# Six scatters of edge features in flight in place of four, and one wait per chunk for layer 1's row gathers

## The reference, cut to what matters

```python
edge_index = stack([src, dst])
x = layernorm(x + L0(x))   # hypergraph convolution: two rounds of two segment sums, relu between
x = layernorm(x + L1(x, edge_attr_64))
x = layernorm(x + L2(x))   # gate = sigmoid(k[dst] + q[src]); segment sum of gate * v[src]
x = layernorm(x + L3(x))   # normalised segment sum of x[col]

# L1, the layer that reads the features of the edges
edge_in = concat([edges, nodes[receivers], nodes[senders]])      # receivers = src, senders = dst
h = relu(edge_in @ We1 + be1)
new_edges = h @ We2 + be2
agg = segment_sum(new_edges, receivers)
new_nodes = relu(concat([agg, nodes]) @ Wn1 + bn1) @ Wn2 + bn2
```

## Time and profile before

| | us |
|---|---|
| median of 3 runs | 4566.49 |
| lowest, highest | 4554.29, 4575.78 |
| the profiled execution, its own time | 4560.08 |
| its span in the profile | 4558.5 |

### The profile page before, as it was taken

How to read it: one execution, slowest core, us unless ns; L and a number is a source line. 1 busy time by engine, 2 the same in 40 slices (tenths; PEclk the granted TensorE clock), 3 DMA queues, 4 the chain that set the end, 5 groups by cost and what they waited for, 6 DMA issues and landing times.

```text
span 4558.5 us, 127255 instructions
## 1 busy us (share of the span) xinstructions
PE 3684.6 (81%) x48218; PEld 3255.3 (71%) x48218; DVE 2888.4 (63%) x3816; ACT 1600.4 (35%) x2668; POOL 2574.3 (56%) x2291
## 2 busy tenths in 40 slices
PE   0777699998899998378999999999766777777396
PEld 0656588887899997357777777777655767767396
DVE  6999888887111102268888888888545666666502
ACT  0333399997000000223333333333224544444200
POOL 0288866666555656677777777777203444444100
PEclk9776799999999999689999999999888999999798
DMA  5611188888999997568888888888517767767596
GB/s 163 241 30 30 43 305 319 322 324 325 340 387 385 418 416 279 172 210 267 273 273 275 272 271 272 274 260 274 190 38 240 264 231 239 252 235 247 166 407 249
DMA packets 430076, 1159.85 MB, mean 254 GB/s; under 512 B 111175, under 2 KB 250422, under 8 KB 422712
## 3 DMA queue, kind: packets, MB, share of 16 engines
q1 hardware_dynamic: 331478, 919.45, 56.8%
q0 software_dynamic: 66016, 114.12, 8.4%
q10 hardware_dynamic: 32256, 121.34, 6.8%
HBM read 791.79 MB, written 364.93 MB: 254 GB/s over the span
## 4 chain that ended last, share of the span: by engine, by line
DMA 33%; issue 25%; POOL 17%; PE 16%; DVE 5%; POOLq 2%; SPq 1%; ACT 1%; DVEq 0%; ACTq 0%
DMA feat_slot<-SK,sidx_p 19%; DMA arena<-tab_l_src,SK 7%; POOL arena L854 7%; POOL feat_slot L930 5%; PE PS L1271 4%; POOL arena L973 4%; PE PS L1396 3%; PE PS L1376 2%; DMA sidx_p<-SK 2%; PE PS L1370 2%; DMA arena<-feat_slot 2%; DMA hots<-arena 1%; PE PS L1365 1%; PE PS L1342 1%; DMA SK<-in_edge_attr_dram 1%
## 5 line engine op out<-in xcount | busy, mean ns | idle before, releaser
L930 POOL DMA_INDIRECT feat_slot<-SK,sidx_p x900 | 1106.8, 1230 | 557.0 <-DMA feat_slot<-SK,sidx_p 283.6
L973 POOL DMA_INDIRECT arena<-tab_l_src,SK x864 | 1007.9, 1167 | 266.8 <-issue 216.8
L854 POOL TENSOR_TENSOR arena<-arena 128x448 f16<-128x448 f32 x343 | 363.2, 1059 | 660.6 <-ACT arena L1730 660.5
L1271 PE MATMUL PS<-arena 128*128 128x192 bf16 (+1 forms) x7203 | 615.6, 248 | 104.3 <-DVE arena L2183 62.2
L1271 PEld LDWEIGHTS PS<-arena 128*128 128x128 bf16 x7203 | 606.7, 98 | 111.7 <-DVE arena L2183 62.5
L1438 PE MATMUL PS<-arena 128*128 128x128 f16 x4802 | 459.8, 223 | 134.4 <-DVE arena L2364 73.8
L1442 PE MATMUL PS<-arena 128*128 (+1 forms) x4802 | 439.0, 195 | 0.1
L1438 PEld LDWEIGHTS PS<-arena 128*128 128x128 bf16 x4802 | 313.1, 99 | 161.8 <-issue 147.4
L2429 DVE TENSOR_TENSOR arena<-arena 128x896 f32<-128x896 f32 (+1 forms) x319 | 328.1, 1028 | 150.3 <-ACT arena L1770 136.7
L1370 PE MATMUL PS<-arena 128*128 (+1 forms) x4178 | 418.6, 224 | 0.0
L1396 PE MATMUL PS<-arena 128*128 128x384 bf16 x2089 | 416.7, 337 | 2.1 <-DVE arena L2436 2.1
(11 more groups left out here) (274 smaller groups left out, 6546.6 us busy)
## 6 DMA issues: line engine op xcount, KB each, us to landing
arena<-slot_rows SPq DMA_DIRECT2D x343, 448.0 KB, 5.6
arena<-cnt_t SPq DMA_DIRECT2D x147, 896.0 KB
hots<-arena ACTq DMA_DIRECT2D x175, 672.0 KB
arena<-hots SPq DMA_DIRECT2D x175, 672.0 KB, 4.3
arena<-cnt_t SPq DMA_DIRECT2D x147, 672.0 KB
cnt_t<-arena SPq DMA_DIRECT2D x49, 1568.0 KB
cnt_s<-arena SPq DMA_DIRECT2D x49, 1568.0 KB
arena<-cnt_s SPq DMA_DIRECT2D x49, 896.0 KB
```

What stands on the lines that cost most here:

```text
L854: pool.tensor_tensor(halves[i][:, n:2 * n], gated[i], halves[i][:, 0:n], ALU.subtract).then_inc(msg_lo, 1)
L930: pool.indirect_dma_start(feat_slot, bass.IndirectOffsetOnAxis(ap=sidx_p[odd][:, n:n + 1].bitcast(u32), axis=0), fwin[h][:, t * D:(t + 1) ...
L973: pool.indirect_dma_start(qgot[n % 3][:, slot_of[t] * P:(slot_of[t] + 1) * P], None, tab_src[4], bass.IndirectOffsetOnAxis(ap=gidx[odd][:, ...
L1271: last = nc.tensor.matmul(PS[:, at:at + w3], ring[u % RING][:, of:of + P], esplit[:, (i * CH + w) * w3:(i * CH + w + 1) * w3], start=u == ...
```

## The change

`LIVE` goes from 4 to 6: six scatters may be in flight, with six semaphores of 6 landings a window each. The gathers of layer 1 get two semaphores in place of six, one for even and one for odd chunks. Before its first gather, a chunk waits once, on the semaphore of its own parity, until the whole chunk two before has landed. The wait before each gather and the empty instruction behind it go, and `add_sources` waits once for the whole chunk.

```diff
-LIVE = 4
+LIVE = 6
 PUTS = WT // LIVE
...
-        q_in = added[4:7] + [gate_in, gate_out, ft_in]
+        q_in = added[4:6]
...
                         if n == 0:
                             pool.wait_ge(gidx_in, j * 16 + 16)
+                        if not first or n >= 2:
+                            pool.wait_ge(q_in[n % 2], (j * NCH + n - n % 2) * (TN * 8))
                         pool.nop(nofuse=True)
                         for t in range(TN):
                             tile = n * TN + t
-                            if not first or n > 0:
-                                pool.wait_ge(q_in[t], j * (NCH * 16) + n * 16)
-                                pool.nop(nofuse=True)
                             pool.indirect_dma_start(qgot[n % 3][:, slot_of[t] * P:(slot_of[t] + 1) * P], None, tab_src[4],
                                                     bass.IndirectOffsetOnAxis(ap=gidx[odd][:, tile:tile + 1].bitcast(u32), axis=0))\
-                                .then_inc(q_in[t], 16)
+                                .then_inc(q_in[n % 2], 16)
...
-                    for t in range(TN):
-                        dve.wait_ge(q_in[t], j * (NCH * 16) + (c + 1) * 16)
+                    dve.wait_ge(q_in[c % 2], (j * NCH + c - c % 2 + 2) * (TN * 8))
```

## The result

The changed kernel takes 4524.69 us, the median of 9 runs (4512.89 to 4544.69); the kernel before, in the same runs, 4559.55 (9 runs, 4552.73 to 4585.29). The ratio is 0.9916, 95% interval 0.9896 to 0.9936: faster by 0.84%, some 38 us (29 to 47); the medians lie 34.9 apart. Forecast were 4512 us, 4490 to 4548, and "faster by over 0.5%" at 82 in 100. The time lies in the range, 13 us above the forecast. The profiled execution took 4529.34 us.

A forecast was written before the change was run, and what follows sets the result against it. The prediction took POOL, issuing gathers end to end, to bound layer 1. Its terms, -56.6 (earlier gathers) + 2 (layer 0) + 0 (gathers' edit) = -54.6 us, took the 4566.5 us median to 4512, range 4490 to 4548.

The forecast's parts named there:

- 1780 to 1880: Sign in the changed kernel's profile: layer 0's scatters end between 1780 and 1880 us.
- the 1814 of the sum: Predicted end of the scatters: near 1944 us less some 130 us of waits that go.
- what the sum took at nothing: Excess scatter waits after 1815 us, and those before 560 us, were not counted as savings.
- only wait longer: Rival: scatters wait their turn behind bulk stores, so six in flight gain 0, time 4566 us; 12 in 100.
- The next thing late: Layer 1's gathers cannot start before its tables are split (`splits_lo`, about 1890.7 us), bounding the gain at 56.6 us.
- layer 0 +2: Term for layer 0: scatters and fetches moved ahead of 1800 us delay it by 2 us.
- the bound of 13: Most that layer 0 loses if loads bound it: some 13 us of transfers moved earlier.
- the 10 us that it named as a sign of being wrong: Sign against the prediction: layer 0 ending more than 10 us later.
- costs nothing: Term for layer 1's gathers: their new chunk-wise wait and the removed waits and empty instructions together change 0 us.
- cover enough: Waiting for the chunk two before leaves 9.1 us of cover, against gather landings of at most 7.4 us.
- to pace layer 1: POOL issues layer 1's gathers end to end and PE follows, so start delays or gains reach the end in full.
- -56.6: Term for the earlier start of layer 1's gathers: 1947.29 - 1890.73 = 56.6 us saved, taken in full.

The follow-up runs named there:

- e3: The changed kernel with a wait and an empty instruction put back before each gather, on the chunk's own semaphore and count: 4527.83 us, ratio 0.9930.
- e7: The changed kernel with a second load of the same source indices per pair, into a tile nobody reads: 4516.07 us (1 run).
- e2: The changed kernel with four scatters in flight in place of six, so the gathers' edit alone: 4572.9 us, ratio 1.0019.
- e1: The kernel before with six scatters in flight in place of four, gathers as before: 4508.39 us, ratio 0.9893.
- e12: The changed kernel with four semaphores for the gathers in place of two, three gathers to each, waits once a chunk: 4501.73 us, ratio 0.9885.
- e5: The changed kernel with twelve semaphores for the gathers in place of two, one for each of up to twelve unfinished: 4513.10 us, ratio 0.9885.
- e4: The changed kernel with the load of the next pair's source indices issued after the fourth chunk in place of the second: 4532.52 us (1 run).
- e10: The changed kernel without the source-index loads from the third pair on, so layer 1's sums differ: 4526.0 us (1 run).
- e11: The changed kernel with three loads of the source indices per pair, two into tiles nobody reads: 4523.38 us (1 run).

## Why the prediction was right, and where it was not

*The scatters.* Right in mechanism and nearly in size. The waits for their own landings nearly go, other waits come in their place, and the last scatter falls inside 1780 to 1880, 24 us earlier than the 1814 of the sum. Most of these 24 us are what the sum took at nothing: behind 1815 the kernel before has another 16 us of waits over the gaps of 0.30 (39.6 us before 79 scatters). That six in flight would "only wait longer" is ruled out by the series 3, 4, 6, 9, in which the time to landing does not grow: the landings seen beside layer 0's loads are latencies that more scatters cover, not the rate at which a full queue serves. From 1400 to 1600 us, where the DMA share reads 1.02, POOL is busy for 135.4 us with scatters where it was 119.0. The Trainium skill (DMA: Bandwidth & Descriptors, "Queues, rings and completion order") has the queues of a DMA engine take turns by packets; the runs do not show the turns, but if there are any they leave room for this.

*The start of the gathers.* The next thing late was the split of the tables, as forecast, and POOL's path to it was shortened past need: of 153.8 us 105.5 end as a wait.

*Layer 0.* The term "layer 0 +2" was too small. Its last reduction comes at 1794.37; in the timeline of before the same one stands at 1787.14, so +7.2; in the other profiles with six or nine scatters in flight it is between 1792.9 (e3) and 1798.0 (e7). That is 6 to 11 us, inside the bound of 13 that the prediction set by the moved transfers, and at its upper end past the 10 us that it named as a sign of being wrong. PE's waits for `cnt_t` from 1110 to 1800 us hardly grew (42.0 to 42.9 us), so the loss is spread thinly and which instruction bears it was not followed.

*The gathers.* This is the step that failed: that the gathers' edit "costs nothing". The prediction asked whether looser waits could let POOL fall behind and found cover enough, and treated the semaphore on which a landing is counted as free. Measured, the edit puts 27 us into the gathers' stretch of the profile, and some 9 to 20 us into the time: 9 by e2's ratio and 13 by the medians of e2 and before, 10 by the ratios of the change and e1 and 16 by their medians, 14 by the ratios of the change and e12, 20 by the spans of the change and e1.

The runs narrow down the cause so far. Shown: it is not the instruction stream (e3) and not the number that may be unfinished (e5, e12, both with twelve and no standstill); with the same chunk-wise wait and the same bound it is there with six gathers on a semaphore and not with three (e12); it stands right behind the load of the indices, moves with it (e4), and is absent without that load (e10) and with two or three of them (e7, e11). Four profiles of four have it with six gathers on a semaphore and one load a pair; each of the kernels without it was profiled once. Open: why POOL stands, and what is counted over three pairs, 108 gathers and 3 loads, so that every third load meets it (all but one in e2). Not shown either is what POOL waits for: in the changed kernel, in the 2 us after it goes on, 17, 3, 2, 0, 1 and 0 landing events of its DMAs come at the six places, where 18 are usual, so in five of six it goes on about when nearly all that it had issued has landed. A simple count of DMAs since the last standstill was the idea behind e7, e10 and e11; it wanted standstills at other distances there, and none came.

*What the standstills cost.* The prediction took POOL to pace layer 1, from the earlier trace rows, and for lost time that holds: the stretch of 1311.3 us is 30 to 31 us longer than in e5 and e12 (1280.9 and 1280.1), which have the same bound of twelve, and the standstills are 29.1. Against before's 1284.6 it is 27. It would not hold for time saved: in e10, relieved of its loads and its standstills, POOL waits for DVE.

*The sum, put right:* -50.5 for the start (layer 0's share in it), +26.7 for the gathers, -7.0 behind them, which is within what that part differs by between profiles. The prediction's own working with 7 for layer 0 gives -56.6 + 7 + 0 = -49.6, and e1, which has no gathers' edit, measured -51. Of the forecast -54.6 the change brought 35 by medians, 38 by the ratio. The step that failed is the "+ 0" for the gathers, with the "+ 2" for layer 0 too small by 5. That the time came out only 13 us above 4512, and not 20, is luck of the base: the median of the three runs shown, 4566.5, lies 7 us above that of the nine.

## What to carry to other kernels

Waits for a transfer's own landing go away with more in flight as long as the landing is latency; count what the next dependency leaves of the gain before you count the waits (here 51 of 157 us), and go no further than that (nine scatters give what six do). Merging the semaphores of many unfinished indirect DMAs was no free simplification here: compare the issuing engine's gaps that the profile puts down to "issue" before and after. The best kernels of this study keep `LIVE` = 6 and have one gather (e1, e5), or three (e12), to a semaphore.

## What the runs showed of the hardware

*Gaps without a wait.* POOL's indirect DMAs follow each other at 0.30 us, with a wait and an empty instruction between them (e3) as without. With six of them on one semaphore and one plain load a pair, POOL stood five or six times for 2.8 to 6.5 us over 864 gathers (the change, e2, e3, e4) at no wait of the program.

*Landings.* A scatter of 32 KB took a median of 4.4 us to land while layer 0's loads ran (DMA share 0.96 in the kernel before and 0.98 in the change from 1140 to 1815 us), with 3, 4, 6 and 9 in flight alike.

*The clock between layer 0 and layer 1.* The stretch 1795 to 1895 us holds the same projections in every kernel with six scatters or more in flight. Here it is in the changed kernel, in e3 and in e5 (after the length: busy us and instructions of PE, PEld, DVE, ACT and POOL, granted clock, DMA share, GB/s):

```profile
1795.00:1895.00 100.00, 46.26 (x399) 45.46 (x396) 46.17 (x50) 33.62 (x43) 0.00 (x0) 0.75 0.28 97
```

```profile
1795.00:1895.00 100.00, 59.01 (x392) 58.40 (x392) 38.50 (x40) 27.74 (x36) 0.00 (x0) 0.65 0.17 57
```

```profile
1795.00:1895.00 100.00, 78.23 (x393) 77.82 (x391) 31.73 (x33) 19.96 (x26) 0.00 (x0) 0.53 0.00 1
```

Nearly the same number of matmuls takes PE 78 us in e5 in place of 46, with a mean granted clock of 0.53, close to the lower level of 1.2 GHz (0.5) for the whole stretch, against 0.75. e3, with 59 us at 0.65, lies between the two (e10 too, 60 us at 0.66), and its first gather came 12 us late. What PE did before was the same: from 1700 to 1785 us e5's PE is busy 82.4 of 85 us at a clock of 1.00 (82.0 in the changed kernel), then it pauses through the layer's end, whose last reduction is at 1796.59 (1797.38 in e1). The first group of 14 at line 1040 behind the pause takes 3.09 us, in the changed kernel and in before 1.77:

```profile
1802.71 3.09 PE L1040 MATMUL PS<-w2x,arena 65*128 65x64 f32 x14
```

So the first gather came at 1936.2, and that execution took 4544.16 us where two others of e5 took 4499 and 4503. Those were not profiled, but their mean clock over the whole run is higher, 0.924 and 0.925 against 0.917. The changed kernel too has two runs in nine at 4544, at 0.921 and 0.922 where the others have 0.923 to 0.927. That these runs are the same thing is likely and not shown. In the kernel before, a delay of this kind would have cost little, since the gathers could not start before 1947: the change has put the projections on the path, and with them their clock.
